# Reordering the opening of a latent attention and ternary FFN block: guard product, weight splits, magnitude sums and X1 rows

## The reference

```python
h = layernorm(x)
Q, V = h @ Wq.T + bq, h @ Wv.T + bv          # 16 heads of 32
logits = Q . latent / sqrt(32)               # 64 per head
w = softmax(top_4(logits))                   # other 60 weights are zero
attn = (w . latent + V) @ Wo.T + bo
x = x + layernorm(attn)
ternary(W): s = mean(|W|) + 1e-8; clip(round(W / s), -1, 1) * s
up, gate = layernorm(x) @ ternary(Wu), layernorm(x) @ ternary(Wg)
x = x + layernorm((silu(up) * gate) @ ternary(Wd))
```

## Time and profile before

| What | Value |
|---|---|
| median of 3 runs | 1056.82 us (1056.31 to 1056.98) |
| the profiled execution | 1054.16 us |
| its span | 1052.3 us |
| PE busy | 970.0 us, 92% of the span |
| DVE busy | 734.1 us, 70% |
| ACT busy | 514.4 us, 49% |
| POOL busy | 542.4 us, 52% |
| granted TensorE clock, mean | 0.976 of full speed |

### The profile page before, as it was taken

The page is one execution under the profiler, slowest core; times in us unless marked ns, Lnnn a source line. Parts: engine busy times, 40 slices in busy tenths (PEclk is TensorE's granted clock), DMA queues, the critical chain, the costliest instruction groups (busy, mean ns, idle before and its releaser), DMA issues.

```text
span 1052.3 us, 17868 instructions
## 1 busy us (share of the span) xinstructions
PE 970.0 (92%) x5738; PEld 471.6 (45%) x5738; DVE 734.1 (70%) x2668; ACT 514.4 (49%) x803; POOL 542.4 (52%) x448
## 2 busy tenths in 40 slices
PE   2654998899999999999999999999999999989997
PEld 2421543335444454445444454445444454435443
DVE  7897689836894768936894768936895669835431
ACT  4787777345454445345453445345553445423321
POOL 3366345664566446664566545664465545632332
PEclk9877999999999999999999999999999999999999
DMA  8934502343024321254023331244022411212001
GB/s 257 404 84 94 154 5 61 80 120 91 12 41 83 78 81 20 40 112 99 10 40 74 86 81 20 40 106 104 10 40 64 96 31 21 41 40 61 1 0 40
DMA packets 149334, 76.94 MB, mean 73 GB/s; under 512 B 135824, under 2 KB 135824, under 8 KB 148112
## 3 DMA queue, kind: packets, MB, share of 16 engines
q1 hardware_dynamic: 149264, 76.18, 29.0%
HBM read 34.21 MB, written 8.39 MB: 40 GB/s over the span
## 4 chain that ended last, share of the span: by engine, by line
PE 74%; DVE 12%; ACT 4%; issue 4%; DMA 3%; POOL 2%; SPq 0%; POOLq 0%; DVEq 0%; ACTq 0%
PE ug L670 36%; PE ug L687 17%; PE ring L536 11%; PE ring L648 7%; PE ring L584 2%; DMA PT<-halves 1%; DVE Lr L1474 1%; DVE v L1452 1%; DVE halves L1432 1%; PE ring L628 1%; DVE ugt L1437 1%; ACT xn L838 1%; DMA x<-in_Wq 1%; DVE stx L1570 1%; DMA X1T<-halves 1%
## 5 line engine op out<-in xcount | busy, mean ns | idle before, releaser
L670 PE MATMUL ug<-X1T,TU 128*128 128x512 f16 (+1 forms) x1152 | 245.1, 356 | 8.4 <-DVE ugt L1442 4.7
L1173 POOL TENSOR_TENSOR hT<-ugt,hT 128x512 f16<-128x512 f32 x128 | 168.0, 1312 | 164.2 <-ACT hT L953 164.2
L670 PE MATMUL ug<-X1T,TG 128*128 128x512 f16 (+1 forms) x1152 | 244.9, 356 | 0.0
L687 PE MATMUL ug<-TD,hT 128*128 128x512 f16 x960 | 214.0, 384 | 3.2 <-issue 3.2
L946 ACT ACTIVATE ugt<-ug,cu 128x512 f32<-128x512 f32 x128 | 87.8, 686 | 207.2 <-PE ug L670 206.3
L670 PEld LDWEIGHTS ug<-X1T,TU 128*128 128x128 f16 x1152 | 110.3, 98 | 117.5 <-issue 5.9
L670 PEld LDWEIGHTS ug<-X1T,TG 128*128 128x128 f16 x1152 | 112.6, 98 | 108.7
L1437 DVE SCALAR_TENSOR_TENSOR ugt<-ugt,ug 128x512 f32<-128x512 f32 x128 | 87.2, 682 | 103.6 <-ACT ugt L946 102.7
L687 PEld LDWEIGHTS ug<-TD,hT 128*128 128x128 f16 x960 | 94.0, 99 | 120.6 <-issue 11.0
L1474 DVE MATCH_REPLACE8 Lr<-v,Lb 128x68 f32<-128x68 f32 x512 | 102.3, 211 | 0.2 <-issue 0.2
L1507 DVE BATCH_NORM_STATS2 stf<-ug 128x6 f32<-128x512 f32 x30 | 20.8, 694 | 109.4 <-PE ug L687 109.4
(11 more groups left out here) (196 smaller groups left out, 1433.5 us busy)
## 6 DMA issues: line engine op xcount, KB each, us to landing
out_dram<-Lr SPq DMA_DIRECT2D x32, 256.0 KB, 3.1
x_in<-in_x SPq DMA_DIRECT2D x7, 1024.0 KB, 5.4
x<-in_x SPq DMA_DIRECT2D x28, 256.0 KB, 3.3
PT<-in_Wd SPq DMA_DIRECT2D x8, 512.0 KB, 7.5
hT<-in_Wu SPq DMA_DIRECT2D x4, 512.0 KB, 10.2
hT<-in_Wg SPq DMA_DIRECT2D x4, 512.0 KB, 15.2
x_in<-in_Wd SPq DMA_DIRECT2D x4, 512.0 KB, 5.3
x_in<-in_x SPq DMA_DIRECT2D x4, 256.0 KB, 3.9
```

Source lines behind the costliest of these rows:

```text
L670: last = pe.matmul(ug[:, 2 * (e % 2) + s, cols], w[:, k, e * P:(e + 1) * P], X1T[:, b, k, cols], start=(k == 0 and b == 0), stop=(k == KD ...
L687: last = pe.matmul(down_bank(kind, t), hT[:, a, e, t * P:(t + 1) * P], td[:, e, :], start=(e == 0 and a == 0), stop=(e == NE - 1 and a == 1))
L1173: pool.tensor_tensor(hT[:, 1, e, :], ugt[:, 2 + e % 2, :], hT[:, 0, e, :], ALU.subtract).then_inc(h_lo, 1)
```

## The change

Only orders change; every instruction that computes is still there, with the same shapes.

- PE: the guard product of g = 1 stands after `logits(0, 1)`, between the halves of Q, instead of after `logits(2, 3)`; its result goes to columns 2 and 3 of bank 3 of `ring` instead of a bank of `ug`. Before it PE waits for all four first halves of Q to be read, and `q_half(3, 1)` waits for the first step of `powers(1)`. `total(weight_sum(0))` stands after `wo(0)` and `wo(1)`. In the second body the total of Wd stands after `upgate(7)` instead of `upgate(6)`.
- DVE: `powers(1)` stands before `maxes(0, 0)`, `weights_lo(1)` after `replace(1, 1)`, `latV_lo` after `replace(2, 1)` and ahead of `weights_lo(2)`. `tern_total(0)`, `tern_scale_of(0)` and `round_to(0)` come later, and the X1 splits `t2_lo` stand among `y_b` and `y_c`, ahead of the roundings.
- ACT: the exponentials come before the weight splits that stood ahead of them, the magnitude sums are dealt out in another order, `sign(0)` moves behind `s1_rows(1, 3)`, and `sign(1)` and `sign(9)` move from the end of the opening to behind `q(3)` of the second body. There `t2_rows(-1, 2)` stands ahead of `q(0)`. `SIGN_AT`, `SUM_AT` and `exp4_at` follow.
- SP: the four transposes `t2(0, t)` stand ahead of the six reloads of Wd pieces.

The diff, cut to its core:

```diff
-        ASUM_ACT = (2, 3, 4, 16, 17, 5, 18, 19, 6, 7) + tuple(range(8, 16)) + tuple(range(20, 24))
+        ASUM_ACT = (16, 17, 18, 19) + tuple(range(2, 16)) + tuple(range(20, 24))
...
-            return (ring, ug)[g][:, 3, 0:2]
+            return ring[:, 3, 2 * g:2 * g + 2]
...                                                  # SP, first body
-                    t2(0, 0)
-                    t2(0, 1)
+                    for t in range(TT):
+                        t2(0, t)
                     wait(sp, vw_done, i, KD, KD)
...
                     down_piece(1, True)
-                    t2(0, 2)
-                    t2(0, 3)
...                                                  # PE, first body
                     logits(0, 1)
-                    for m in range(1, KD):
-                        q_half(m, 1)
+                    pe.wait_ge(qa32_ready, KD)
+                    total(guard_sums(1), mg[:, 2:4], mg_ready, 2, ma_ready)
+                    q_half(1, 1)
+                    q_half(2, 1)
+                    pe.wait_ge(sc_step, 7)
+                    q_half(3, 1)
                     logits(2, 3)
-                    wait(pe, l_ready, i, 8, 4)
-                    total(guard_sums(1), mg[:, 2:4], mg_ready, 2, ma_ready)
                     for m in range(KD):
                         v(m)
                     weigh_half(0)
+                    wo(0)
+                    wo(1)
                     wait(pe, l_ready, i, 8, 8)
                     total(weight_sum(0), tot[:, 0:1], tot_ready, 1, tota_ready)
-                    wo(0)
-                    wo(1)
...
-                    if kind == "second" and e == 6:
+                    if kind == "second" and e == 7:
                         total(ring[:, bank_of("S", 0, 0), 0:1], tot[:, 2:3], tot_ready, 3, tota_ready)
...                                                  # ACT, second body
+                if kind == "second":
+                    t2_rows(-1, 2)
+                    q(0)
+                    t2_rows(-1, 3)
+                    for m in range(1, KD):
+                        q(m)
                     sign(1)
                     sign(9)
+                    act.wait_ge(tern_ready, after_tern(1, 9))
...
-                SIGN_AT = {0: (5,), 1: (13, 3), 2: (11,), 3: (6,), 4: (14,), 8: (22, 23), 9: (16, 17), 11: (7, 15), 12: (20, 21), 14: (18,)}
-                SUM_AT = {2: (4,), 3: (5, 6), 4: (7,)}
-                exp4_at = (5, 9, 13) if late else (3, 6, 11, 15)
+                SIGN_AT = {0: (2,), 1: (10,), 2: (5, 13), 3: (3, 11), 4: (6,), 5: (14,), 8: (22, 23), 9: (16, 17), 11: (7, 15), 12: (20, 21), 14: (18,)}
+                SUM_AT = {2: (4,), 3: (5,), 4: (6, 7)}
+                exp4_at = (4, 9, 13) if late else (3, 6, 11, 15)
...                                                  # DVE, first body, end
                     t2_lo(0, 0)
                     y_a(3)
+                    y_b(2)
                     t2_lo(0, 1)
+                    y_c(0, 2)
+                    y_b(3)
+                    t2_lo(0, 2)
+                    y_c(0, 3)
                     round_to(1)
-                    y_b(2)
-                    y_b(3)
                     round_to(9)
-                    y_c(0, 2)
-                    y_c(0, 3)
+                    t2_lo(0, 3)
                     round_to(4)
...
                     round_to(13)
-                    t2_lo(0, 2)
-                    t2_lo(0, 3)
```

More of the change, by code:

```diff
@@ L975, in body @@
                     logits(1)
+                    exp4(0)
                     weights_hi(1)
-                    exp4(0)
+                    exps(0)
                     latV_hi()
[L979 to L986, removed]
                     abs_sum(16)
                     abs_sum(17)
-                    exps(1)
+                    exp4(1)
+                    probs_hi(0)
+                    logits(2)
+                    abs_sum(18)
+                    weights_hi(2)
+                    exps(1)
+                    abs_sum(19)
+                    abs_sum(2)
+                    abs_sum(3)
+                    exp4(2)
+                    abs_sum(4)
                     abs_sum(5)
-                    abs_sum(18)
-                    abs_sum(19)
                     probs_hi(1)
+                    logits(3)
                     abs_sum(6)
                     abs_sum(7)
-                    exp4(2)
-                    logits(3)
+                    exps(2)
                     abs_sum(8)
-                    abs_sum(9)
[L1000 to L1004, removed]
+                    exp4(3)
+                    vw_half(0, 0)
+                    vw_half(1, 0)
+                    vw_half(2, 0)
+                    vw_half(3, 0)
+                    probs_hi(2)
+                    exps(3)
+                    abs_sum(9)
                     abs_sum(10)
                     abs_sum(11)
-                    exps(3)
                     abs_sum(12)
-                    abs_sum(13)
                     probs_hi(3)
@@ L1012, in body @@
                     s1_rows(1, 1)
+                    abs_sum(13)
                     abs_sum(14)
                     abs_sum(15)
-                    sign(0)
-                    for m in range(KD):
-                        vw_half(m, 1)
+                    vw_half(0, 1)
+                    vw_half(1, 1)
+                    vw_half(2, 1)
+                    vw_half(3, 1)
                     s1_rows(1, 2)
                     s1_rows(1, 3)
+                    sign(0)
                     t2_rows(0, 0)
@@ L1022, in body @@
                     t2_rows(0, 1)
+                    return
+                if kind == "second":
[4 more added lines that the diff above has]
+                        q(m)
                     sign(1)
                     sign(9)
[L1025 to L1029, removed]
+                    act.wait_ge(tern_ready, after_tern(1, 9))
+                else:
+                    for m in range(KD if att else 0):
+                        q(m)
+                        if m < 2:
+                            t2_rows(-1, 2 + m)
                 if kind == "second":
@@ L1052, in body @@
                         keep_residual()
+                    if e in exp4_at:
+                        exp4(exp4_at.index(e))
                     for n in SIGN_AT.get(e, ()) if late else ():
@@ L1056, in body @@
                         abs_sum(2 * NPIECE + q)
-                    if e in exp4_at:
-                        exp4(exp4_at.index(e))
                     if e in exps_at:
@@ L1603, in body @@
                     abs_sum(1)
+                    powers(1)
                     maxes(0, 0)
@@ L1608, in body @@
                     replace(0, 1)
-                    powers(1)
                     maxes(1, 0)
@@ L1612, in body @@
                     sums(0)
-                    weights_lo(1)
                     select(0)
@@ L1617, in body @@
                     replace(1, 1)
-                    latV_lo()
+                    weights_lo(1)
                     maxes(2, 0)
@@ L1625, in body @@
                     replace(2, 1)
+                    latV_lo()
                     weights_lo(2)
-                    tern_total(0)
                     maxes(3, 0)
@@ L1635, in body @@
                     ln1_stat(1)
+                    tern_total(0)
+                    sums(3)
+                    select(3)
+                    y_a(0)
+                    ln1_biases(1)
+                    y_a(1)
                     tern_scale_of(0)
                     round_to(0)
[L1638 to L1642, removed]
                     y_b(0)
```

2 lines of the change are left out of this document (removed).

## The result

The changed kernel took 1049.14 us (median of 4 runs, 1048.09 to 1050.87) against 1056.65 (1056.31 to 1056.98): ratio 0.9931, 95% interval 0.9918 to 0.9944, 7.5 us less. The forecast was 1054.2, its range began at 1051.8: the direction was right, but the gain is three times the one forecast. The profiled execution took 1049.91, so 4.25 us less than the profiled one of before (1054.16).

The account below looks back on a forecast made before the run. Limits in turn: the softmax chain, PE and ACT at the seam, then DVE. Seam terms -0.65 and -2.07 make -2.7, -2.6 remaining after the ACT and DVE stretch: 1056.8 - 2.6 = 1054.2 us, range 1051.8 to 1057.4.

Parts of the forecast that it names:

- Part 1: Opening, guard product and `powers(1)` early: `powers(1)` takes 1.1 us, `maxes(0)` 0.8 us late, `maxes(1)` 2.0 us earlier.
- Parts 2 and 3: Opening: exponentials first bring `select(0)` 5.0 us earlier; the Wv split, 6.2 us beside POOL, pays that back by `maxes(2)`.
- Part 4: Opening, `latV_lo` and Wo split: `maxes(3)` 0.7 us earlier, `weigh_half(1)` at 90.6; term -0.65 us.
- Each taking turns with the split of Wo: it ends at 65.1: Opening: POOL's `probs_lo(1)` and `shift(2)` alternate with DVE's Wo split, which ends at 65.1 against 65.8.
- the first rival: DVE keeps the port at the Wv and Wo splits, ahead of POOL: -3.9 us, 1052.9; chance 0.14 together with no blocking.
- Part 5: Seam, X1 rows: earlier transposes remove PE's wait for X1, -2.07 us, with 3 us to spare.
- Part 6: Second body, ACT order: `hidden(5)` at 142.0, `upgate(7)` at 143.4; 2.6 us earlier in all stays on DVE.
- both waits: Second body: DVE's `hidden(5)` behind sums awaiting `exp4(0)`, and PE's 1.52 us at the Wd total, both go.
- The sum's last line: Whole kernel: the median's 2.66 us above the profiled execution carries over, so 1051.6 becomes 1054.2 us.
- Time won before that point is kept to the end: From about 260 us on PE is busy nearly throughout, so time won earlier is kept.
- The slower rival: Second body: `t2_rows(-1, 3)` starts late on ACT and delays `q(3)`; +2.1 us, 1058.9; chance 0.12.
- the one in which ACT takes the gain back: Second body: two added signs cost 2.1 us in ACT's full stretch, leaving 0.5 us gain, 1056.3; chance 0.20.

Follow-up runs that it names:

- Part 1 alone: The kernel before with only the guard product behind `logits(0, 1)` and `powers(1)` ahead of `maxes(0, 0)` (also called guard alone): 1053.43 us against 1056.32, ratio 0.9979.
- The one-line experiment that restores the turns: The changed kernel with only `latV_lo` moved from behind `replace(2, 1)` to ahead of `select(1)`: 1050.05 us, ratio 0.9938.
- the slower profile of before: The kernel before, unchanged, profiled a third time: 1057.04 us.
- both kernels with the 3.42: The kernel before with Part 5 only, 1054.27 us; the changed kernel with second-body `exp4(0)` and Wd total both put back, 1052.48 us.
- X1 alone: The kernel before with only the X1 transposes, rows and splits earlier and their table of signs: 1054.27 us against 1056.55, ratio 0.9984.

## Why the forecast was wrong

- **Part 1** held: `powers(1)` took 1.11 us (forecast 1.1) and ended at 31.61, corrected 30.7 (30.8). What I had not seen is its worth by itself: alone it moves the whole chain by 3.2, since it brings ACT's `exp4(0)` forward as well.
- **Parts 2 and 3** held: corrected by the 0.9 of the late loads, `select(0)` is at 39.6 (forecast 39.85), the split of Wv takes 6.28 (6.2), `maxes(2)` starts at 50.4 (50.8). That the new place of this split pays back the exponentials' gain is shown: in its old place the kernel is 1.9 us faster. It pays back more than that: with Part 1 alone `weigh_half(1)` comes 1.0 us earlier than with Parts 1 to 4.
- **Part 4 failed in its size.** "Each taking turns with the split of Wo: it ends at 65.1" - it ended at 60.9, corrected. Turns were seen only where POOL's instruction was under way or began with the first of the four, and `probs_lo(1)`, which I had at 59.9, 1.2 us into them, could not get in between. I had put the same rule on both places without asking who starts first. Part was lost again: `shift(2)` now ran beside `sums(2)`, whose 16-element instruction took 1.73, and `select(2)` waited 0.80 for its exponential. Term: -2.2 in place of -0.65. The one-line experiment that restores the turns takes 0.9 of these 1.6 us away again at `weigh_half(1)` (2.4 in the median of that comparison); another 0.5 was there when the split began (58.2, corrected, for 58.7). Of the first rival this is the half at Wo; at Wv its condition did not hold.
- **Part 5** was right on the trace that I read (the wait of 2.07 is gone) and too small for the kernel: in the slower profile of before the wait is 4.80 and what follows it runs at half clock.
- **Part 6** was right in place and too small. I had `hidden(5)` at 142.0 and -2.6 in all after this stretch; it came at 139.3, corrected, and -5.5. Of these 2.9 us the opening had brought 1.9 (with `logits(0, 1)` at -4.6, not -2.7), the stretch itself 1.0. What I called both waits going was an edge: without that exponential one row earlier, the 1.5 us wait becomes 3.42 (or one of 4.48 behind it), with half clock in part of what follows. An earlier seam does not do this (guard alone: 1.53); both kernels with the 3.42 have the two signs of Part 5 ahead of a late `exp4(0)`.
- **The sum's last line failed as well, by about as much.** I carried the 2.66 us between the profiled execution and the median of before over to the kernel after. But the median of the changed kernel is 0.77 below its profiled execution, whose loads came 0.9 late: with these taken off, the distance is 0.1. The wait at half clock, which most of the 2.66 fits (3.1 us at `logits(0, 1)`), goes with the change, as the granted clocks of the single runs bear out. Of the 5.1 us by which 1054.2 missed 1049.14, about 2.5 are this step, and 2.6 the terms on the path: 2.9 by Parts 4 to 6, less the 0.3 lost after `down(0)`.
- **"Time won before that point is kept to the end"** held only to within some 3 us. From `down(0)` to the end the profiled executions take 861 to 864 us, and the changed kernel itself 862.6, 862.7 and 864.0; no run shows why.

The slower rival and the one in which ACT takes the gain back did not happen: `t2_rows(-1, 3)` began at 108.81, not at 115.84, and ACT's two more signs were covered. The latter is, however, what X1 alone showed, where they were not: `exp4(0)` came 2.5 us later against the logits, and the time fell by 2.3 us only.

Shown by runs, as differences of medians: the exponential (3.5 to 3.7 us with the rest in place), the guard product (2.9 alone), X1 (2.5 with the rest in place, 2.3 alone), the place of `latV_lo` (0.9 to 2.4, by the median of the changed kernel that it is set against) and of the split of Wv (-1.9). The parts are not a sum: each fills room that another opened. Left open: why Q sometimes runs at full clock in before and sometimes not, and that most runs of before have the long wait; one profile of three shows it, the rest is inferred from their times and granted clocks.

## What to carry to other kernels

Read at least two executions of the kernel before, one of them near the median, before a term is read off a wait: what divides them may be the very thing that the change removes. Price a wait of PE with what follows it, and ask of every saving which wait is next and what may grow into it, here two signs moved ahead of an exponential. Try each part alone: the first gave more in the opening than Parts 1 to 4 together. Before placing a run of DVE instructions beside POOL, look at who will start first.

## What the runs showed of the hardware

- Four DVE instructions with two SBUF inputs (128x512, 2.65 us alone) took 6.28 beside POOL where POOL's instruction began 0.08 or 0.16 us after the first of them, 5.98 where it had begun 0.36 before, and 2.73 where it began 1.31 after; then POOL's took 3.42. The Trainium skill, page "SBUF — State Buffer", section "Who interferes with whom", says that a DVE instruction with two SBUF inputs contends with a GpSimd instruction that reads SBUF, and that issue order decides who is blocked. The traces agree, and add that a run of DVE instructions already under way can keep POOL out to its end.
- Even a small DVE instruction can be held: the TENSOR_SCALAR on 128x16 elements in `sums` takes 0.17 us alone and up to 1.67 to 1.88 beside a POOL `shift` of 1.93. The reduction just ahead of it was not: 0.22 us at 141.35, with the `shift` under way since 141.32.
- After PE waits of 3.42 to 4.97 us, what follows ran in part at half clock, 1.2 GHz (1.87 for 1.03; 3.60 for 1.89), after 2.07 not; but after one of 2.40 in the guard-alone kernel it did. The length of the wait alone does not decide it.
